# A fused two-layer adaLN kernel on one core: sums over states taken transposed, the gate moved to position by channel, halves further overlapped, states taken downwards in every second block

## The reference

```python
xz = jnp.einsum('btd,de->bte', x, in_proj_w)
x_branch, z = jnp.split(xz, 2, axis=-1)
...
A_bar = jnp.exp(dt[..., None] * A[None, None])
Bx = dt[..., None] * B_t[:, :, None, :] * x_branch[..., None]
def step(h, inp):
    a, bx, c = inp
    h = a * h + bx
    y = jnp.einsum('bds,bs->bd', h, c)
    return (h, y)
...
y = y + D_param[None, None, :] * x_branch
y = y * jax.nn.silu(z)
return jnp.einsum('btd,de->bte', y, c_proj_w)
```

## Time and profile before

| | us |
|---|---|
| median of three runs | 1267.32 |
| the profiled execution, first to last instruction (span) | 1264.5 |
| PE busy | 1140.8 |
| DVE busy | 1155.2 |
| ACT busy | 795.0 |
| POOL busy | 982.6 |
| mean DMA rate | 248 GB/s |

### The profile page before, as it was taken

The page is one execution under the profiler, slowest core; times in us unless marked ns, Lnnn a source line. Parts: engine busy times, 40 slices in busy tenths (PEclk is TensorE's granted clock), DMA queues, the critical chain, the costliest instruction groups (busy, mean ns, idle before and its releaser), DMA issues.

```text
span 1264.5 us, 12574 instructions
## 1 busy us (share of the span) xinstructions
PE 1140.8 (90%) x3612; PEld 640.1 (51%) x3612; DVE 1155.2 (91%) x1138; ACT 795.0 (63%) x1445; POOL 982.6 (78%) x712
## 2 busy tenths in 40 slices
PE   7989678998999899997999899997999899789996
PEld 5636333664457444764457443763457443444453
DVE  3768999999999999899999999899999999999987
ACT  2256567765786668755786668755786667655532
POOL 3216886889778887989778997889778996976862
PEclk9999989999999999999999999999999999899998
DMA  7308588766868688866878679876868786899922
GB/s 285 115 16 315 176 269 284 278 233 233 281 226 297 200 278 292 289 233 225 290 219 301 197 277 311 276 241 217 292 217 287 215 282 236 290 335 346 374 86 116
DMA packets 92309, 313.87 MB, mean 248 GB/s; under 512 B 10432, under 2 KB 15680, under 8 KB 91984
## 3 DMA queue, kind: packets, MB, share of 16 engines
q1 hardware_dynamic: 89936, 306.26, 70.3%
q10 hardware_dynamic: 2304, 6.82, 1.5%
HBM read 301.73 MB, written 11.31 MB: 248 GB/s over the span
## 4 chain that ended last, share of the span: by engine, by line
PE 43%; DVE 22%; POOL 14%; ACT 9%; issue 8%; DMA 3%; SPq 0%; DVEq 0%; POOLq 0%; ACTq 0%
PE ps L907 13%; DVE ps L1741 12%; POOL arena L1970 8%; PE ps L601 5%; PE ps L830 4%; PE ps L609 3%; DVE arena L1749 3%; DMA arena<-bc_scratch 2%; PE ps L647 2%; PE ps L751 2%; PE ps L723 2%; ACT ps L1295 2%; ACT arena L931 2%; PE ps L728 1%; PE ps L633 1%
## 5 line engine op out<-in xcount | busy, mean ns | idle before, releaser
L1970 POOL TENSOR_TENSOR arena<-arena 128x1024 f32<-128x1024 f32 x255 | 600.3, 2362 | 136.5 <-PE ps L907 113.2
L1741 DVE TENSOR_TENSOR_SCAN ps<-ps,arena 128x1024 f32<-128x1024 f32 (+1 forms) x257 | 585.8, 2280 | 30.3 <-ACT ps L1295 17.9
L907 PE MATMUL ps<-arena,identF 128*128 128x512 f32 x1024 | 482.8, 603 | 49.0 <-DVE arena L1749 29.4
L1295 ACT ACTIVATE ps<-arena,negA 128x512 f32<-128x512 f32 x512 | 332.7, 683 | 83.2 <-DVE arena L1749 78.2
L907 PEld LDWEIGHTS ps<-arena,identF 128*128 128x128 f32 x1024 | 190.3, 193 | 267.2 <-issue 208.8
L1749 DVE TENSOR_TENSOR arena<-ps,arena 128x1024 f32<-128x1024 f32 (+1 forms) x257 | 312.0, 1214 | 5.9
L922 ACT ACTIVATE arena<-arena,rnln 128x256 f32<-128x256 f32 x118 | 61.9, 589 | 42.1 <-POOL rnln L1776 24.9
L647 PE MATMUL ps<-arena,inw 128*128 128x512 f32 x128 | 60.0, 614 | 11.7 <-ACT arena L931 9.6
L1307 ACT ACTIVATE arena<-ps 128x2 f32<-128x2 f32 x128 | 22.0, 172 | 64.9 <-DVE arena L1749 64.4
L931 ACT ACTIVATE arena<-ps,modT 128x512 f32<-128x512 f32 x43 | 51.7, 1266 | 14.7 <-PE ps L474 12.6
L728 PE MATMUL ps<-arena,inw 128*128 128x512 f32 x128 | 60.2, 592 | 0.0
(11 more groups left out here) (222 smaller groups left out, 1707.1 us busy)
## 6 DMA issues: line engine op xcount, KB each, us to landing
arena<-bc_scratch SPq DMA_DIRECT2D x511, 512.0 KB, 5.0
arena<-in_x SPq DMA_DIRECT2D x16, 256.0 KB, 6.9
arena<-in_x SPq DMA_DIRECT2D x8, 512.0 KB, 8.4
xr_scratch<-arena SPq DMA_DIRECT2D x6, 512.0 KB, 6.9
px_scratch<-arena SPq DMA_DIRECT2D x6, 512.0 KB, 6.1
out_x<-arena SPq DMA_DIRECT2D x5, 512.0 KB, 2.6
arena<-bc_scratch SPq DMA_DIRECT2D x9, 256.0 KB, 3.6
woT<-in_woT SPq DMA_DIRECT2D x4, 512.0 KB, 10.0
```

Source lines behind the costliest of these rows:

```text
L907: x = pe.matmul(ps[:, Y, :], identF[:], inp[:, m % RING, q, :], start=False, stop=(i == BLOCK_STEPS - 1 and q == 1), skip_group_check=True)
L1295: x = act.activation(ps[:, 2 * (m % 2) + q, :], dt[:, kd, :], ACT.Exp, scale=negA[:, kd, 2 * i + q:2 * i + q + 1])
L1741: x = dve.tensor_tensor_scan(states, states, inp[:, m % RING, q, :].rearrange("p q t -> p (q t)"), 0.0, ALU.mult, ALU.add)
L1970: x = pool.tensor_tensor(inp[:, m % RING, :, :], u[:, kd:kd + 1, :].broadcast_to([P, 2, TH]), b_at[:, m % 3, :, :], ALU.mult)
```

## The change

1. **Transposed sums.** The sums over states are no longer matmuls with the identity as weights. Each 128x128 piece of a product is loaded as weights and the identity streams through in transpose mode, accumulating in bank Y: 4 transposes for each 128x512, positions by channels. D times x enters Y by 4 matmuls of 128x128 with a diagonal matrix of D as moving operand (`pe_dx`), which takes ACT's write (L1318) out; SP loads the diagonal of the next block (64 KB) once a block. The very last block of the kernel is summed as before (`direct`).
2. **The gate position by channel.** `pe_z` takes 8 matmuls of 128x128 in place of 2 of 128x512 and leaves z positions by channels. DVE's product with the gate is the same instruction on the transposed tiles. It must be turned back for the output projection: `pe_back`, 4 transposes into Y0, and `act_back`, an ACT copy of 128x512, once per block but the last.
3. **States downwards.** In every second block the pairs of states are taken from 7 down to 0 (`pair_of`), so a block starts with the rows that the one before ended with. `row_places` keeps them: of the 256 row loads of each kind, 184 of B (3 places) and 208 of C remain. C has 2 places instead of 3, and its load waits for the product two steps back. Of 512 row loads 392 are left.
4. **Overlapped halves.** The norm of the quantized projection's input and of the third layer norm go to other tiles (`hB3`, `hn3b` in the convolution's buffer), so attention of half h+1 may start before half h has left its convolution: the first transposes of `pe_before` wait for `ffn_tmp` instead of `bc_sb` and `xc`. The whole table `TIMES` has new numbers, with entries of its own for turning back. Some semaphores are merged.

DVE and POOL execute the same number of instructions of each kind and size as before.

```diff
-    "pe_before": {"hn1_t0": -2.25, "hn1_t1": -2.25, "q0": -2, "k0": -2, "s0": 2, "q1": 2, "k1": 3.75, "v0": 5.25,
...
+    "pe_before": {"hn1_t0": -10.75, "hn1_t1": -10, "q0": -18.5, "k0": -13.5, "s0": 2.75, "q1": -14.75, "k1": 4.25,
...
+def row_places(slots):
+    held, used, count, places = [None] * slots, [-1] * slots, [0] * slots, []
+    for m in range(G * STEPS):
+        rows = (m // STEPS, pair_of(m))
+        fresh = rows not in held
+        at = min(range(slots), key=lambda n: used[n]) if fresh else held.index(rows)
+        assert not fresh or used[at] <= max(m - slots, -1)
+        held[at], used[at], count[at] = rows, m, count[at] + fresh
+        places.append((at, fresh, count[at]))
+    return places
+def pair_of(m):
+    r = m % BLOCK_STEPS
+    return BLOCK_STEPS - 1 - r if m // BLOCK_STEPS % 2 else r
...
         def sp_scan(step, quarter):
-            m = step + 2
-            if quarter == 0 and 0 <= m < G * STEPS:
-                h, kd, i = at_step(m)
-                if m >= 3:
-                    sp.wait_ge(S.prod, m - 2)
...
+            m = step + 2
+            if quarter == 2 and 0 <= m < G * STEPS and c_rows[m][1]:
+                h, i, at = m // STEPS, pair_of(m), c_rows[m][0]
+                if m >= 2:
+                    sp.wait_ge(S.prod, m - 1)
...
+            n = step // BLOCK_STEPS + 1
+            if quarter == 3 and step % BLOCK_STEPS == 2 and 0 < n < KD * G - 1:
+                sp.wait_ge(S.dx, n)
+                sp.dma_start(d_diag, d["d_diag"][:, n % KD, :]).then_inc(S.dd_in, 16)
...
         def pe_before(h):
...
             yield t + T["hn1_t0"]
-            pe.wait_ge(S.bc_sb, h)
             pe.wait_ge(ln["ln1"].hn, 2 * h + 2)
+            if h > 1:
+                pe.wait_ge(S.ffn_tmp, 2 * (h - 1) - 1)
+            else:
+                pe.wait_ge(S.bc_sb, h)
...
         def pe_z(h, kd):
-            for k in range(KE):
-                x = pe.matmul(ps[:, z_bank(h, kd), :], inw[:, k, DI + kd * P:DI + (kd + 1) * P], hB3[:, k, :],
-                              start=(k == 0), stop=(k == KE - 1))
+            own = slice(DI + kd * P, DI + (kd + 1) * P)
...
+                for j in range(JH):
+                    for k in range(KE):
+                        x = pe.matmul(ps[:, z_bank(h, kd), j * P:(j + 1) * P], hB3[:, k, j * P:(j + 1) * P], inw[:, k, own],
+                                      start=(k == 0), stop=(k == KE - 1))
             x.then_inc(S.z_mm, 1)
+        def pe_back(n):
+            pe.wait_ge(S.gated, n + 1)
+            for j in range(JH):
+                x = pe.transpose(ps[:, Y0, j * P:(j + 1) * P], sz[:, n % KD, j * P:(j + 1) * P], identF[:])
+            x.then_inc(S.yb, 1)
...
+        def pe_add_transposed(src, last):
+            for j in range(JH):
+                x = pe.matmul(ps[:, Y, j * P:(j + 1) * P], src[:, j * P:(j + 1) * P], identF[:], start=False,
+                              stop=last, is_transpose=True, skip_group_check=True)
+            return x
+        def pe_dx(n):
+            pe.wait_ge(S.xc, min(n + 2 - n % 2, KD * G))
+            pe.wait_ge(S.dd_in, 16 * (n + 1))
+            if n:
+                pe.wait_ge(S.gated, n)
+            for j in range(JH):
+                x = pe.matmul(ps[:, Y, j * P:(j + 1) * P], xc_of(n // KD, n % KD)[:, j * P:(j + 1) * P], d_diag, start=(j == 0),
+                              stop=False, skip_group_check=True)
+            x.then_inc(S.dx, 1)
...
+        def act_back(n):
+            act.wait_ge(S.yb, n + 1)
+            act.activation(y2T[:, n % KD, :], ps[:, Y0, :], ACT.Copy).then_inc(S.yt, 1)
```

More of the change, by code:

```diff
@@ L1840, in pool_before @@
             xrow = xrows[h % 3]
+            yield t + T["ln1_rstd"]
+            pool_rstd("ln1", h)
             if h % 2 == 0:
@@ L2019, in layout @@
         "cpw": cols(a["L1_attn_c_proj_w"]),
+        "d_diag": np.zeros((P, KD, P), np.float32),
     }
+    own = np.arange(P)
+    out["d_diag"][own, :, own] = vec(a["L1_attn_D_param"])
     for g in "fico":
```

271 lines of the change are left out of this document (163 added, 108 removed), and 14 rows, old and new, of the table TIMES.

## The result

The change made the kernel slower: 1286.06 us median (4 runs, 1284.04 to 1287.3) beside 1268.13 (1266.7 to 1269.87), a ratio of 1.0135, interval 1.0123 to 1.0147. Forecast were 1233 us and a range that ends at 1262. The profiled execution took 1286.13 us, its span is 1284.8.

The account below looks back on a forecast made before the run. VectorE and TensorE, both near 94% in a middle half, wait for each other in turn. Span 1264.5 - 32.6 (middle) - 3.5 (97.5 to 200 us) + 2 (row loads) = 1230.4; the median lies 2.8 above: 1233 us, range 1215 to 1262.

Parts of the forecast that it names:

- The costs of TensorE: TensorE's work in a middle half: sums -26.9, z +4.4, D times x +5.6, turning back +1.8; 134.4 to 119.3 us.
- what becomes of the waits in the middle: VectorE's idle 50.2 us in the middle: decays 13.3, POOL's products 11.1, gate 5.5, rest 2.7 won; together 32.6 us.
- My fifth rival: Nothing changes, since VectorE's waits have other causes than TensorE: 1267 us, chance 0.03.
- more can be ahead in time; what is gained is in the shares above: Overlapped halves and new order: no gain or loss of their own beyond the shares of waits already counted.
- half, 3.5: From 97.5 to 200 us, VectorE's idle 6.6 us has the middle's causes; half of it, 3.5 us, won.
- the start before the first scan and the end after 1200 keep their chains: Before the first scan and after 1200 us: the same chains, so nothing won or lost.
- Row loads: Fewer row loads, with C's load issued later: costs 2 us over the whole kernel, bounds 0 and 14.
- my bound of 14: Upper bound for C's later loads in the row-load term: 23 loads x 0.6 = 14 us.
- VectorE's 1155.2 us "stay": Whole kernel: VectorE executes the same instructions of the same sizes, so its busy time stays 1155.2 us.
- The clock (1 and 2): Transposes lower TensorE's clock: after each long stretch, 1257 us, chance 0.17; or most of the time, 1305 us, chance 0.08.
- Serial waits through bank Y0: Turning back adds four round trips to a shared bank; with C's loads at 14 us, 1250 us, chance 0.08.
- signs that I had named for a wrong forecast: VectorE's instructions longer, start or end changed by more than 3 us, or decays late although TensorE is free.

Follow-up runs that it names:

- e18: The kernel before, order and loads untouched, with each identity sum cut to its first 128 of 512 columns: 1274.5 us.
- e10: The change with the old numbers for both chains beside the first 32 steps (second half's preparation; first half's z, copies back, gates): 1270.5 us.
- e9: The change with C's rows in three places, loaded earlier and ahead of B's; the identity replaces the diagonal of D: 1285.9 us.
- e11: The change with the edits of both e9 and e10: 1266.3 us.
- e4: The kernel before with only the downward states and the fewer row loads, C in two places: 1286.9 us.
- e8: e4 with three places for C, its loads issued as before, a step earlier and ahead of B's: 1269.44 us.
- e13: The change without turning back the gated sums (no transposes or copies back); what follows reads them untransposed: 1282.9 us.
- e16: The change with the start of e10, keeping only one of the four transposes of each half-sum: 1263.9 us.
- e3: The change's transposed sums and row loads in the old order, with the old numbers and waits: 1321.0 us.
- e15: e10 with C's load ahead of B's in SP's queue, C still in two places: 1270.8 us.

## Why the prediction was wrong

**The costs of TensorE were right.** Transposed sums at 0.11 us a piece, z, D times x and the way back gave 119.3 us a half; measured are 120.7, 118.5 and 122.9. The accumulating transposes cost what the plain ones cost: 8 in 1.04 to 1.09 us at the full clock, as in the earlier trace rows.

**Where the 54.4 us went** between the forecast span, 1230.4 us, and the measured 1284.8: 26.5 in blocks 4 to 25 (32.6 forecast for 200 to 1100 us, 6.1 won), 23.4 until block 3 ends (3.5 forecast as won, 19.9 lost), 6.6 in the last six blocks (nothing forecast), less the 2 that I had put down for the row loads and 0.1 at the end.

**The step that failed first: what becomes of the waits in the middle.** I let 32.6 us follow TensorE's work, by shares (85% of the decays, 90% of POOL's products, the gate, a quarter of the rest). POOL's and the gate's went about as computed. The decays' 13.3 did not go at all (11.8 before, 13.6 after, in blocks 4 to 25); the wait for z grew by 5.5; C's rows brought 5.8. Between the ends of blocks 3 and 25 VectorE's idle time fell from 43.9 to 37.0 us; less 0.8 of longer instructions that is the 6.1 won. The shares had no row behind them: a wait that ends with ScalarE was put down to TensorE because some of ScalarE's waits end there. e18 shows that this is no property of the change: before, too, shorter sums in that order gave nothing, at a clock of 0.87. What holds the decays and z in the change is not shown. My fifth rival said just this ("VectorE's waits have other causes than TensorE") and had 0.03.

**The step that turned a small gain into a loss: "more can be ahead in time; what is gained is in the shares above", with "half, 3.5" for 97.5 to 200.** That the start before the first scan and the end after 1200 keep their chains was nearly right: the first scan begins at 100.47 us for 97.57, and from the last gate to the end it is 41.7 for 41.8. The new order puts other work beside the first 32 steps, which are steps like no others, since there is no half before them. It costs 7.2 us until block 0 ends and 12.7 in the next three, and e10 gives 16 of the 20 back. I had looked at the new order in a middle half only. The last six blocks lose 6.6, since VectorE there has 1.8 us more to do and idles 10.8 for 6.0; no run in the new order mends that, and its cause is open.

**Row loads.** +2 was about right for the change (0 in e9, 4 in e11 beside e10), but by luck: in the old order the same edit costs 17 (e4 beside e8), beyond my bound of 14. The mechanism that I named, a landing against a scan, a product and a scan, fits: C's loads land in 4.8 us at the median and 12.0 at the longest in e4, and VectorE waits for 25 of them. But they are late throughout, 19.9 of the 26.9 us between 200 and 1100, where I had looked at the last scans.

**VectorE's 1155.2 us "stay".** They became 1162.7. Four copies of 128x12 took 1496 ns on average where they took 392, which is 4.4 us, and at the start one product took 2277 ns for 683 and another 1.52 us for 0.69; together 6.8 of the 7.5. All of the long ones began while POOL was in an instruction of its own that reads SBUF, and the one copy of after that did not took 0.14 us; before the first scan:

```profile
95.88 2.36 POOL L1898 TENSOR_TENSOR arena<-arena,gbias 128x1024 f32<-128x1024 f32 x1
97.27 1.52 DVE L1678 TENSOR_TENSOR arena<-arena 128x512 f32<-128x512 f32 x1 [0.25 <-DMA arena<-bc_scratch]
99.74 0.69 DVE L1678 TENSOR_TENSOR arena<-arena 128x512 f32<-128x512 f32 x1 [0.95 <-DMA arena<-bc_scratch]
```

The first of the two equal products ends 0.55 us after POOL's, a little less than one product's length; the second, with POOL idle, takes 0.69. The 2277 ns one, too, ends 0.55 us after a product of POOL. The Trainium skill (SBUF — State Buffer, "SBUF: two separate sides") says that an operation of VectorE with two SBUF inputs and one of GpSimd that reads SBUF exclude each other for a whole instruction; by that rule a new order changes VectorE's own time, and the trace agrees for the two products. The copies have one SBUF input, so this sentence does not cover them.

**The rivals.** The clock (1 and 2) fell as forecast in kind: 0.95 from 200 to 1100 us. But 1257 and 1305 rested on it being the price, and at that clock a half's work was 118.5 to 122.9 for 119.3; it was dearer in e18, 15 us a half. *Serial waits through bank Y0* had a mechanism that is there (ScalarE waits 35.9 us for turning back, 200 to 1100 us) and is worth 6 us of the middle and 3 of the whole by e13, a small part. No rival ended above 1267 us by an order that fits the start badly, which is what happened. Three of the signs that I had named for a wrong forecast came: longer instructions of VectorE, a start more than 3 us off, and decays that stay late.

## What to carry to other kernels

Where engines in a fixed order wait for each other in turn, do not take what shortening one of them is worth from the waits beside it (32.6 us here, of which 6.1 came). A kernel with that work simply left out says more (e18 gained nothing); it is a one-line edit and should come before the real one, read together with its clock. Look at a new order in its first and last rounds as well as in a middle one, and cut both traces at the same events, not at the same times. What a buffer place is worth depends on the order around it: taking one from C cost 17 us in the old order, and nothing to 4 in the new one, while the traffic saved was worth nothing.

## What the runs showed of the hardware that I had not expected

The clock fell where TensorE still did some work, if only transposes. TensorE in the change at the start, in order of time:

```profile
151.25 0.66 PE L791 MATMUL ps<-identF,arena 128*128 128x128 f32 x4 [1.79 <-DVE arena L1579]
152.38 1.09 PE L975 MATMUL ps<-identF,arena 128*128 128x128 f32 x8 [0.47 <-DVE arena L1866]
155.84 1.97 PE L975 MATMUL ps<-identF,arena 128*128 128x128 f32 x8 [2.37 <-DVE arena L1866]
...
171.44 1.97 PE L975 MATMUL ps<-identF,arena 128*128 128x128 f32 x8 [10.17 <-DVE arena L1866]
174.91 1.97 PE L975 MATMUL ps<-identF,arena 128*128 128x128 f32 x8 [1.50 <-DVE arena L1866]
```

Eight transposes take 1.09 us at the higher level of the clock, 2.4 GHz, and 1.97 at the lower, 1.2. The kernel before lost its clock here after 0.09 us of work in 3.4 and had it back a few microseconds later, with identity sums; the change keeps the low one over bursts of transposes, and from 150 to 175 us its clock is 0.60 for 0.86. The Trainium skill (TensorE: Matmul & The Clock Gate, "Part 4: PE-mode transpose") says that transposes don't count as busy in the way matmuls do. The rows fit that but do not show it by themselves, since the stretch also holds 10.2 us of idle time, and transposes are not needed for it: e18 has only shorter identity sums, and its clock in the middle is 0.87 where the change's is 0.97. I had weighed the clock as a matter of transposes alone, and the runs do not bear that out. Nor do they give another rule: e16 has a clock of 0.91 with 583.84 us of work in 769.2, e18 0.87 with 616.67 in 789.5.

A low clock can cost little: e3 has 0.64 from 150 to 175 us and loses 1.4 us by block 3, and e15 has 0.80 in blocks 1 to 3 where the change has 0.78, with 8 us between them.
